# Mamba layer of a four-layer tower: GpSimd weights the states by C in every fourth turn, from a broadcast row; five state buffers, five pieces of B's rows

## The reference

```
def step(hst, ins):
    d_t, B_t, C_t, u_t = ins
    dA = jnp.exp(d_t[..., None] * A)
    hst = dA * hst + (d_t * u_t)[..., None] * B_t[:, None, :]
    y = jnp.einsum('bds,bs->bd', hst, C_t)
    return (hst, y)
...
y = ys.transpose(1, 0, 2) + u * Dp
y = y * jax.nn.silu(z)
return y @ out_w.T
```

## Time and profile before

| | |
|---|---|
| median of the runs | 3571.7 us |
| lowest of the runs | 3560.6 us |
| the profiled execution | 3563.0 us, its span 3561.2 us |
| busy in the span | PE 2552.1 us, DVE 2422.7, ACT 1601.1, POOL 838.6 |
| rounds of `mamba_stage` | about 677 to 1395 us of the span |
| mean granted TensorE clock | 0.831 of full speed |

### The profile page before, as it was taken

The page is one execution under the profiler, slowest core; times in us unless marked ns, Lnnn a source line. Parts: engine busy times, 40 slices in busy tenths (PEclk is TensorE's granted clock), DMA queues, the critical chain, the costliest instruction groups (busy, mean ns, idle before and its releaser), DMA issues. The chain is left out here.

```text
span 3561.2 us, 39662 instructions
## 1 busy us (share of the span) xinstructions
PE 2552.1 (72%) x13085; PEld 1555.3 (44%) x13132; DVE 2422.7 (68%) x5748; ACT 1601.1 (45%) x2888; POOL 838.6 (24%) x446
## 2 busy tenths in 40 slices
PE   3968995788888876699831112789889777776357
PEld 3955663333434333489721111323222266665335
DVE  4454335399999997211388997687787689999531
ACT  1111112566666652111116772677777545555211
POOL 1000000477676772267300000000000001111022
PEclk9767997799999997799955555899999889887668
DMA  1121001101010100511100000100000100000131
GB/s 37 19 80 45 1 1 31 63 33 70 26 63 33 58 37 0 159 43 40 51 10 1 1 1 1 56 1 1 1 1 1 53 23 1 1 1 1 58 134 54
DMA packets 61429, 114.90 MB, mean 32 GB/s; under 512 B 32685, under 2 KB 50188, under 8 KB 55884
## 3 DMA queue, kind: packets, MB, share of 16 engines
q1 hardware_dynamic: 55084, 100.16, 8.3%
q0 software_dynamic: 6144, 12.25, 1.1%
HBM read 98.31 MB, written 21.99 MB: 34 GB/s over the span
## 5 line engine op out<-in xcount | busy, mean ns | idle before, releaser
L1943 POOL TENSOR_TENSOR mam_st<-mam_du,mam_b_rows 128x1536 f32<-128x1536 f32 x128 | 439.5, 3440 | 172.8 <-PE mam_ysum L2012 172.3
L2173 DVE TENSOR_TENSOR_SCAN mam_st<-mam_da,mam_st 128x512 f32<-128x512 f32 x384 | 441.1, 1204 | 35.9 <-ACT mam_da L2113 18.2
L1721 DVE TENSOR_TENSOR cod_hp<-cod_hp,cod_gate 128x512 f32<-128x512 f32 x512 | 324.0, 681 | 122.2 <-ACT cod_hp L1588 122.0
L2012 PE MATMUL mam_ysum<-mam_st,held_ident 128*128 128x512 f32 x768 | 390.0, 648 | 2.2 <-DVE mam_st L2179 2.2
L1588 ACT ACTIVATE cod_hp<-cod_up,cod_b 128x512 f32<-128x512 f32 x512 | 318.8, 692 | 130.2 <-PE cod_up L1459 129.8
L2113 ACT ACTIVATE mam_da<-mam_delta,mamw_decay 128x508 f32<-128x508 f32 x384 | 254.2, 683 | 184.2 <-DVE mam_st L2173 149.5
L2294 POOL TENSOR_TENSOR att_probs<-att_se,att_neg 128x1536 f32<-128x1536 f32 x16 | 55.0, 3438 | 997.0 <-DVE att_neg L2499 997.0
L2179 DVE TENSOR_TENSOR mam_st<-mam_st,mam_c_ps 128x1536 f32<-128x1536 f32 x128 | 224.4, 1753 | 16.9 <-PE mam_c_ps L2007 13.4
L2012 PEld LDWEIGHTS mam_ysum<-mam_st,held_ident 128*128 128x128 f32 x768 | 159.8, 208 | 167.9 <-issue 160.8
L489 DVE SCALAR_TENSOR_TENSOR held_h<-x_dn,held_gate,held_h 128x192 f32<-128x192 f32 x256 | 89.1, 410 | 183.6 <-PE x_dn L456 181.9
L1464 PE MATMUL cod_gate<-cod_wt,cod_sel_g 128*128 128x512 bf16 x465 | 182.2, 392 | 39.0 <-DVE cod_hp L1721 38.4
(11 more groups left out here) (525 smaller groups left out, 5477.0 us busy)
## 6 DMA issues: line engine op xcount, KB each, us to landing
mam_b_rows<-b_scratch SPq DMA_DIRECT2D x32, 1024.0 KB, 8.0
slot_scratch<-in_slot_fresh SPq DMA_DIRECT2D x2, 3860.0 KB
sw_w<-in_L_w SPq DMA_DIRECT2D x1, 6144.0 KB, 18.6
gr_w<-in_L_w SPq DMA_DIRECT2D x1, 5376.0 KB, 42.2
gr_w<-in_L_w SPq DMA_DIRECT2D x1, 4608.0 KB
sw_w<-in_L_w SPq DMA_DIRECT2D x1, 4608.0 KB, 31.3
gr_rows<-slot_scratch SPq DMA_DIRECT2D x40, 96.5 KB, 1.9
x1w_w<-in_L_w SPq DMA_DIRECT2D x1, 3072.0 KB
```

The lines of the kernel that those rows point to most:

```text
L1721: nc.vector.tensor_tensor(at, at, gate[u % BANKS][:], ALU.mult).then_inc(gated, 1)
L1943: nc.gpsimd.tensor_tensor(st[it % N_ST][:], du[r % 2][:], along(b_rows[:, p % RING, n % PIECE, :], 1, [P, MC, MT]), ALU.mult)\
L2012: last = nc.tensor.matmul(ysum[:, c, :], m.ident[:], st[it % N_ST][:, c, :], start=False, stop=(it % DS == DS - 1))
L2173: nc.vector.tensor_tensor_scan(fs, fa, fs, 0.0, ALU.mult, ALU.add).then_inc(scanned, 1)
```

## The change

GpSimd takes step 5 in the turns with it % 4 = 1 (n = 1, 5, 9, 13 of each round). For these, TensorE no longer spreads C's row. GpSimd cannot read PSUM, so SP loads that row, on all partitions, from DRAM: the scratch transfer (L1894) carries 32 rows of `dbl` (C's 16 and B's 16) where it had B's 16, and a ring `c_rows` of 3 rows of 512 is filled with one 128x512 transfer for each piece of B. The weighting of turn `it` stands in GpSimd's queue behind the drive of turn it + 3 (`POOL_LAG`). `N_ST` goes from 4 to 5, `RING` from 6 to 5. The sums of a turn wait for whichever engine weights it.

```diff
--- before.py
+++ after.py
@@ -1810,8 +1810,10 @@
 C_ROWS, B_ROW, DT_ROW = (0, 32, 64), 16, 96
 CP = 96
 PIECE = 4
-RING = 6
-N_ST = 4
+RING = 5
+C_RING = 3
+POOL_AT, POOL_LAG = 1, 3
+N_ST = 5
 USES = [10 if r % 2 else (12 if r else 10) for r in range(ROUNDS_M - 1)] + [0]
 IN_AT = 0
 Z_USE, OUT_USE = 7, 10
@@ -1819,6 +1821,18 @@
 
 def uses_before(r):
     return sum(USES[:r])
+
+
+def on_pool(it):
+    return it % PIECE == POOL_AT
+
+
+def pool_count(it):
+    return (it + PIECE - 1 - POOL_AT) // PIECE
+
+
+def dve_count(it):
+    return it - pool_count(it)
 
 
 def conv_use(r):
@@ -1842,6 +1856,7 @@
         delta = [s.sb(f"delta{i}", [P, MC, MT]) for i in range(2)]
         du = [s.sb(f"du{i}", [P, MC, MT]) for i in range(2)]
         b_rows = s.sb("b_rows", [P, RING, PIECE, MT])
+        c_rows = s.sb("c_rows", [P, C_RING, MT])
         st = [s.sb(f"st{i}", [P, MC, MT]) for i in range(N_ST)]
         ys = s.sb("ys", [P, 2, MC, MT])
         spare = m.xw[:].rearrange("p t d -> p (t d)")[:, 0:NB * D].rearrange("p (k c t) -> p k c t", k=2, t=MT)
@@ -1858,8 +1873,16 @@
          dbl_kept, c_rest_ready, c_mid_ready, c_low, b_out, exp_soft, soft_ready, delta_ready,
          du_ready, drive_ready, exp_ready, scanned, c_ready, weighted, summed, finished) = (s.sem(n) for n in names)
         piece_in = [s.sem(f"piece_in{i}") for i in range(RING)]
+        c_row_in = [s.sem(f"c_row_in{i}") for i in range(C_RING)]
+        pool_weighted = s.sem("pool_weighted")
         n_w = 10
         block = s.block()
+
+        def wait_weighted(eng, it):
+            if on_pool(it):
+                eng.wait_ge(pool_weighted, pool_count(it + 1))
+            else:
+                eng.wait_ge(weighted, dve_count(it + 1))
 
         def wait_pre(eng, g):
             if g == 0:
@@ -1891,15 +1914,20 @@
                 sp.wait_ge(dbl_kept, r + 1)
                 if r >= 2:
                     sp.wait_ge(drive_ready, DS * (r - 1))
-                sp.dma_start(m.b_scratch[r % 2], dbl[B_ROW:B_ROW + DS, :]).then_inc(b_out, 16)
+                    sp.wait_ge(pool_weighted, DS // PIECE * (r - 1))
+                sp.dma_start(m.b_scratch[r % 2], dbl[0:B_ROW + DS, :]).then_inc(b_out, 16)
                 sp.wait_ge(b_out, 16 * (r + 1))
                 for q in range(DS // PIECE):
                     p = r * DS // PIECE + q
                     if p >= RING:
                         sp.wait_ge(drive_ready, PIECE * (p - RING + 1))
                     sp.dma_start(b_rows[:, p % RING].rearrange("p n t -> p (n t)"),
-                                 m.b_scratch[r % 2, q * PIECE:(q + 1) * PIECE, :]
+                                 m.b_scratch[r % 2, B_ROW + q * PIECE:B_ROW + (q + 1) * PIECE, :]
                                  .rearrange("n t -> (n t)").partition_broadcast(P)).then_inc(piece_in[p % RING], 16)
+                    if p >= C_RING:
+                        sp.wait_ge(pool_weighted, p - C_RING + 1)
+                    sp.dma_start(c_rows[:, p % C_RING, :], m.b_scratch[r % 2, q * PIECE + POOL_AT, :]
+                                 .partition_broadcast(P)).then_inc(c_row_in[p % C_RING], 16)
 
         @block.gpsimd
         def _(pool):
@@ -1923,6 +1951,13 @@
                 pool.wait_ge(delta_ready, r + 1)
                 wait_u(pool, r)
                 nc.gpsimd.tensor_tensor(du[r % 2][:], delta[r % 2][:], u[r % 2][:], ALU.mult).then_inc(du_ready, 1)
+
+            def weight(it):
+                q, x = it // PIECE, st[it % N_ST]
+                pool.wait_ge(scanned, MC * (it + 1))
+                pool.wait_ge(c_row_in[q % C_RING], 16 * (q // C_RING + 1))
+                nc.gpsimd.tensor_tensor(x[:], x[:], along(c_rows[:, q % C_RING, :], 1, [P, MC, MT]), ALU.mult)\
+                    .then_inc(pool_weighted, 1)
 
             nc.gpsimd.memset(u_pre[:], 0.0).then_inc(padded, 1)
             c_residue(0)
@@ -1943,17 +1978,23 @@
                     nc.gpsimd.tensor_tensor(st[it % N_ST][:], du[r % 2][:],
                                             along(b_rows[:, p % RING, n % PIECE, :], 1, [P, MC, MT]), ALU.mult)\
                         .then_inc(drive_ready, 1)
+                    if it >= POOL_LAG and on_pool(it - POOL_LAG):
+                        weight(it - POOL_LAG)
                     if r + 1 < ROUNDS_M:
                         late = 3 if r % 2 else 0
                         if n == 6 + late:
                             c_residue(r + 1)
                         if n == 9 + late:
                             pool.wait_ge(drive_ready, it + 1)
+                            pool.wait_ge(pool_weighted, pool_count(it - POOL_LAG + 1))
                             c_lowest(r + 1)
                         if n == 11 + late - r % 2:
                             to_delta(r + 1)
                         if n == 12 + late - r % 2:
                             to_du(r + 1)
+            for it in range(NIT - POOL_LAG, NIT):
+                if on_pool(it):
+                    weight(it)
 
         @block.tensor
         def _(pe):
@@ -2000,14 +2041,16 @@
 
             def spread_c(it):
                 r, n = it // DS, it % DS
-                pe.wait_ge(weighted, it)
+                if on_pool(it):
+                    return
+                pe.wait_ge(weighted, dve_count(it))
                 if n == 0:
                     pe.wait_ge(c_mid_ready, r + 1)
                     pe.wait_ge(c_low, r + 1)
                 nc.tensor.matmul(c_ps[:], pick[:, n, :], c_part[r % 2][:], start=True, stop=True).then_inc(c_ready, 1)
 
             def sums(it):
-                pe.wait_ge(weighted, it + 1)
+                wait_weighted(pe, it)
                 for c in range(MC):
                     last = nc.tensor.matmul(ysum[:, c, :], m.ident[:], st[it % N_ST][:, c, :], start=False,
                                             stop=(it % DS == DS - 1))
@@ -2173,8 +2216,10 @@
                 nc.vector.tensor_tensor_scan(fs, fa, fs, 0.0, ALU.mult, ALU.add).then_inc(scanned, 1)
 
             def weight(it):
+                if on_pool(it):
+                    return
                 v.wait_ge(scanned, MC * (it + 1))
-                v.wait_ge(c_ready, it + 1)
+                v.wait_ge(c_ready, dve_count(it) + 1)
                 x = st[it % N_ST]
                 nc.vector.tensor_tensor(x[:], x[:], along(c_ps[:], 1, [P, MC, MT]), ALU.mult).then_inc(weighted, 1)
 
@@ -3293,7 +3338,7 @@
         m.prob_max = s.sb("prob_max", [P, NB])
         m.chosen = s.sb("chosen", [P, NB, 8])
         m.scratch = nc.dram_tensor("heads_scratch", [NB, H0, P, HD0], F32).ap()
-        m.b_scratch = nc.dram_tensor("b_scratch", [2, DS, MT], F32).ap()
+        m.b_scratch = nc.dram_tensor("b_scratch", [2, 2 * DS, MT], F32).ap()
         m.slot_scratch = nc.dram_tensor("slot_scratch", [NT3 * P, XW], F32).ap()
         m.home_scratch = nc.dram_tensor("home_scratch", [2 * T + NT3 * P, D], F32).ap()
         m.key_scratch = nc.dram_tensor("key_scratch", [NB, P], F32).ap()
```

## The result

The changed kernel takes 3615.8 us in the median of its runs (3611.3 to 3624.1), the kernel before 3569.1 in the same comparison. Of its four runs one took 8737.3 us, in a slow state, and is left out of the ratio; the other three took 3560.6, 3566.5 and 3571.7. The ratio is 1.014, 95% interval 1.0128 to 1.0153: about 50 us longer, and within the 2% of the prediction. The span of the profiled execution is 3614.0 us against 3561.2, so +52.8 us, at a mean granted clock of 0.823 (0.831 before).

The account below looks back on a forecast made before the run. VectorE was taken to set the pace, with TensorE full in the convolution turns and ScalarE in turn 9 of even rounds. 3563.0 + 30.4 for the rounds + 13 for the slow clock gave 3606 us, range 3558 to 3634.

Parts of the forecast that it names:

- the steps laid out by hand: Turn-by-turn times of GpSimd, TensorE, ScalarE and VectorE in the rounds, summing to +30.4 us without the slow clock.
- The clock term: TensorE's sums run slower after idling: 1.2 us for each of 11 late sums, +13 us in all, bounds 0 and 19.
- 11 late sums: TensorE's sums delayed by GpSimd's weightings: 3 x 2 + 2 in the even rounds and 3 in the odd.
- Round 0: No outputs in turn 11, so 0.9 us lost there, then turn 13 waits 1.5: 4.5 us longer.
- Odd rounds: Rounds 1, 3, 5: turn 13's weighting stands behind six instructions on GpSimd, its sums come late; 4.1 us longer each.
- Round 7: The last round has no preparation, so all four weightings moved save 1.71 us each: 6.8 us shorter.
- VectorE's waiting for C's row: Sign in the profile: grows from 13.4 to some 50 to 70 us, single waits of 2 to 7 us.
- The edits costed at nothing: C's row loaded by SP and ring 5 for 6 stay hidden; the fifth state buffer only helps; no time added.
- no late sums: Rival (a): GpSimd finishes its weightings in time, so the kernel gets faster, 3530 us; chance 0.15.
- a delay of the odd rounds that is absorbed: Rival (b): the next round's turns absorb the odd rounds' delay and no slow clock, 3581 us; chance 0.15.
- The lock of VectorE against GpSimd: Rival (d): VectorE stands still for 109 us of GpSimd work, less 54.7, 3617 us without late sums; chance 0.02.
- rival (c): Every late sums and dt product at 1.2 GHz, ScalarE's chain pushed again, late `finish`: 3632 us and above; chance 0.10.

Follow-up runs that it names:

- e9: Changed kernel with zero-weight products filling TensorE's waits ahead of the sums of turns 5 and 9 in even rounds; 3606.2 us, 1.0111 of the kernel before.
- e8_warm: Changed kernel with 50 unused products on TensorE ahead of the sums of turn 13 in rounds 1, 3 and 5; 3613.0 us, 1.0139 of before.
- e2_free_turns: Changed kernel with GpSimd weighting only turns 1, 13 of even rounds, 1, 5, 9 of odd, 1, 5, 9, 13 of the last; 3555.2 us, 0.9969 of before.
- e11_best: Changed kernel with GpSimd weighting only turn 13 of even rounds and turns 1, 5, 9, 13 of round 7; 3562.9 us, 0.9982 of before.
- e4: Changed kernel, all 32 weightings, with GpSimd's queue reordered so weightings of turns 5, 9 and odd rounds' 13 stand earlier; 3558.2 us, 0.9982 of before.
- e5: Changed kernel with TensorE's sums of a GpSimd turn one turn later, behind C's row of turn s+2; 3595.0 us, 1.0088 of before.
- e6: Changed kernel with both GpSimd's weightings earlier in its queue and TensorE's sums one turn later; 3568.8 us, 1.0000 of before.
- e7: Changed kernel with GpSimd weighting only turn 13 of rounds 1, 3 and 5; 3595.9 us, 1.0083 of before.
- e10: Changed kernel with GpSimd weighting only turn 5 of the four even rounds; 3604.6 us, 1.0101 of before.

## Why the prediction was right, and where its sizes were off

The forecast was 3606 and slower by 43 us; measured are 50 by the ratio, 52.8 by the spans and 54.0 in the rounds. The mechanism is the one laid out, and the steps laid out by hand, which hold nothing for the clock yet, can be put beside the trace of rounds 2 and 3 (us from the round's first scans):

| step | forecast | changed kernel | full clock (e9) |
|---|---|---|---|
| GpSimd's weighting of turn 5 ends | 40.0 | 39.8 | |
| decays of turn 8 | 46.3 | 48.9 | |
| scans of turn 10 | 61.6 | 64.2 | 61.6 |
| GpSimd's weighting of turn 9 ends | 67.9 | 70.5 | 68.0 |
| VectorE's weighting of turn 11 | 74.9 | 80.2 | 75.7 |
| even round in all | 97.8 | 102.8 | 98.4 |
| GpSimd's weighting of turn 13 ends, odd round | 85.9 | 86.0 | |
| odd round in all | 90.7 | 92.3 | |

GpSimd's side was right to 0.2 us as long as nothing slow stood ahead of it. With the clock held up the walk hits turn 10 exactly and the round to 0.6, which is about the overrun of the filling. So what was mis-sized is in the main one term:

**The clock term** was taken as 1.2 us for each of 11 late sums with bounds of 0 and 1.7, from rows in which sums after 2.18 us of idle time are listed with 4.44 instead of 2.74. After the 4.2 to 12.9 us of idle time that they have in the changed kernel, the 11 late sums are listed with 4.24 to 5.49, so 1.5 to 2.75 more and 2.3 in the mean, above the upper bound: a row from a shorter idle time was no bound for a longer one. What e9_warm_even gets back is 15.4 us for 8 late sums, 1.9 each, and e8_warm 1.4 to 2.0 for each of its three. For 11 that is some 21 us instead of 13 (an estimate). It also falls on sums that the walk has in time, as e2_free_turns shows, and there it was put at nothing. TensorE: Matmul & The Clock Gate in the Trainium skill (Part 1, the clock gate) has the array at 1.2 GHz after idling; the trace agrees for all 11 late sums, none of which is listed with less than 4.24 us, and the clock in the three stretches read around them is 0.67, 0.51 and 0.62 of full. The rule as the prediction took it, each of the 11 paying the upper end of the term, gives +49 and would have come nearer than the middle that was chosen.

**Round 0** was forecast 4.5 longer plus two clock losses, 6.9, and is 11.9. Up to turn 4 it loses 1.6: the sums of turn 1 wait 2.28 us for GpSimd in the first convolution turns and are listed with 4.54, and C's row of turn 3 is waited for 4.61 us where it was 0.36, which the forecast did not lay out. Turn 11 waits 3.65 where 0.9 was said; its sums are listed with 5.49, 2.75 too long.

**Odd rounds** were forecast at +4.1 and the clock's 1.2; by first scans round 3 is 5.6 longer. Right to 0.3, though the 1.71 us counted as gained in turn 9 is in part waited for again in turn 11 (1.1 to 1.7 us), for the reason that e2_free_turns shows.

**Round 7** was forecast 6.8 shorter. It is 8.8 shorter by `finish`; e2_free_turns and e11_best, where no late round stands before it, give 6.7.

**VectorE's waiting for C's row** is 97.3 us where 50 to 70 were forecast. The 11 places that the forecast names hold 69 of it: 18.6 in turns 7 and 25.2 in turns 11 of even rounds, 25.1 in turns 15 of odd ones. Single waits reach 9.1 and not 7; the longest stands behind sums listed with 5.49. The other 28 us are 19 waits in other turns, such as turns 2 and 3 of round 0 (2.77 and 4.61, where before they were 3.66 and 0.36).

**The edits costed at nothing** cost nothing: buffers alone are 0.9999, durations of the instructions are unchanged, and none of GpSimd's waits in the rounds is for a transfer of C's row. **The rivals**: no late sums (3530) are refuted by the 26 waits of 120.8 us, and a delay of the odd rounds that is absorbed (3581) by those rounds, each 4.2 to 7.3 us longer. The lock of VectorE against GpSimd is refuted by scans of 1196 to 1224 ns beside 32 weightings. SBUF — State Buffer in the Trainium skill (two separate sides) names no conflict with GpSimd for a VectorE instruction with at most one input in SBUF, outside its two-port modes, and the trace agrees with scans of 1198 ns in the median in both kernels. The result lies between the forecast and rival (c), which had the slow clock for every late sums right; its late `finish` did not come (4.5 us of waiting in all, less than the 7.4 before).

The forecasts of the experiments were worse than that of the change, and all on one side: each that removed a wait was to give 12 to 36 us more than it gave (e2, e4, e5, e6, e11), and the two that added one kind of late turn (e7, e10) cost 9 and 17 us more than forecast. The first counted 1.71 us for each turn that was made free, and there the trace shows another engine a fraction behind: ScalarE from turn 8 to 10 of even rounds (4.46 us of waiting), TensorE in the convolution turns, and sums slowed by the clock ahead of C's row.

## What to carry to other kernels

An engine that waits a quarter of the time (172 of 718 us here) has room on average only; before moving work to it, write out what stands ahead of the new instruction in its queue at each place, and ask which in-order queue waits for the result and what stands behind it there. Here the same 32 instructions cost 50 us in one order on GpSimd and nothing in another. And a stage in which two other engines are full in places gives back little of what the slowest one saves: only the round without preparation kept its four times 1.7 us. Last, a matrix engine that is made to wait costs more than the wait: price the instructions behind it by a row after a wait as long as the one expected, also where the wait itself harms nobody.

## What the runs showed of the hardware that was not expected

Work that computes nothing can shorten a round: 18 matmul instructions that add zero, set into two waits, raised the granted clock around them from 0.67 and 0.51 to 1.00 and took about 4 us off a round of 102, with no other change in the round. The rows also say how much one wait can cost behind itself: six matmuls take 5.39 us after 4.58 us of idle time, so the wait of 4.58 was in effect one of 7.2. But the idle time alone does not say it. In the kernel before, two sums of round 2 stand behind nearly the same idle time, one turn apart, and one is listed long and the other not:

```profile
934.22 0.39 PE L2007 MATMUL mam_c_ps<-mam_c_part,mamw_pick 96*128 96x512 bf16 x1 [2.16 <-DVE mam_st L2179]
934.45 2.74 PE L2012 MATMUL mam_ysum<-mam_st,held_ident 128*128 128x512 f32 x6
939.37 0.39 PE L2007 MATMUL mam_c_ps<-mam_c_part,mamw_pick 96*128 96x512 bf16 x1 [2.19 <-DVE mam_st L2179]
939.60 4.44 PE L2012 MATMUL mam_ysum<-mam_st,held_ident 128*128 128x512 f32 x6
```
